# Row maxima and causal mask in one tile written by GpSimd, in a Flamingo block of cross-attention and mixture of experts

## The reference: what is computed

```python
q = proj(query, w_q, b_q); k = proj(key, w_k, b_k); v = proj(value, w_v, b_v)
scores = einsum('bhqd,bhkd->bhqk', q, k) / sqrt(D_K)
scores = where(mask, scores, -inf)            # mask: j <= i for sequences of 128
attn = softmax(scores, axis=-1)
out = einsum('bhqk,bhkd->bhqd', attn, v) ... @ w_o.T + b_o
x = x + tanh(g_xattn[0]) * out
x = x + tanh(g_ffn[0]) * experts(layernorm(x))
```

## Time and profile before

| | before |
|---|---|
| median of 3 runs | 963.27 us (963.25 to 963.42) |
| the profiled execution | 958.71 us, its span 956.9 us |
| granted clock of PE, mean | 0.952 |
| PE busy | 849.2 us (89%) |
| DVE busy | 603.9 us (63%) |
| ACT busy | 442.7 us (46%) |
| POOL busy | 258.1 us (27%) |
| mask product, L911 | 128 instructions, 49.1 us busy |

### The profile page before, as it was taken

The page is one execution under the profiler, slowest core; times in us unless marked ns, Lnnn a source line. Parts: engine busy times, 40 slices in busy tenths (PEclk is TensorE's granted clock), DMA queues, the critical chain, the costliest instruction groups (busy, mean ns, idle before and its releaser), DMA issues. The chain is left out here.

```text
span 956.9 us, 25073 instructions
## 1 busy us (share of the span) xinstructions
PE 849.2 (89%) x7600; PEld 752.0 (79%) x7601; DVE 603.9 (63%) x1521; ACT 442.7 (46%) x962; POOL 258.1 (27%) x239
## 2 busy tenths in 40 slices
PE   3699999999999999997258999999899989999990
PEld 2588888888888888886147888989799879889980
DVE  2458888888888888876625555555455545555550
ACT  2354555555555555554034454444445525544440
POOL 2101333323222233232301232332223322323222
PEclk9799999999999999998569999999999989999995
DMA  9767977878787878775878333233323322332212
GB/s 185 153 133 178 204 201 192 185 170 186 177 188 204 199 199 198 179 217 210 282 285 301 52 57 52 48 49 50 60 35 58 51 43 45 50 51 36 29 24 25
DMA packets 90231, 125.38 MB, mean 131 GB/s; under 512 B 13088, under 2 KB 81824, under 8 KB 85920
## 3 DMA queue, kind: packets, MB, share of 16 engines
q1 hardware_dynamic: 74752, 103.95, 42.3%
q0 software_dynamic: 14304, 19.15, 12.7%
q10 hardware_dynamic: 1088, 1.11, 0.4%
HBM read 55.21 MB, written 42.75 MB: 102 GB/s over the span
## 5 line engine op out<-in xcount | busy, mean ns | idle before, releaser
L1195 POOL DMA_INDIRECT out_rows<-yg,xs x78 | 126.6, 1623 | 349.7 <-ACT yg L1237 216.0
L1319 PE MATMUL bank<-xh,wts 128*128 128x256 f16 x1872 | 216.5, 277 | 0.0
L1335 PE MATMUL bank<-wts,hh 128*128 x1872 | 210.6, 273 | 0.0
L1319 PEld LDWEIGHTS bank<-xh,wts 128*128 x1872 | 186.2, 100 | 23.8
L1335 PEld LDWEIGHTS bank<-wts,hh 128*128 128x128 f16 x1872 | 183.2, 98 | 21.2
L1227 ACT ACTIVATE hf<-bank,b1t,gscale 128x256 f32<-128x256 f32 x312 | 154.9, 561 | 24.0 <-PE bank L1319 21.1
L935 PE MATMUL bank<-va,probs 128*128 128x102 f32 x1024 | 140.7, 279 | 7.9 <-DVE ao L653 7.9
L935 PEld LDWEIGHTS bank<-va,probs 128*128 128x128 f32 x1024 | 125.0, 193 | 10.6 <-DVE ao L653 7.4
L1237 ACT ACTIVATE yg<-yb,xs 128x256 f32<-128x256 f32 x78 | 35.4, 500 | 204.2 <-DVE yb L1276 183.1
L541 ACT ACTIVATE probs<-bank 128x512 f32<-128x512 f32 x128 | 76.8, 600 | 102.4 <-PE bank L918 96.7
L1266 DVE SCALAR_TENSOR_TENSOR hh<-hf,hscale,hh 128x512 f16<-128x512 f32 x156 | 117.2, 751 | 5.6
(11 more groups left out here) (169 smaller groups left out, 1108.2 us busy)
## 6 DMA issues: line engine op xcount, KB each, us to landing
wts<-in_W SPq DMA_DIRECT2D x16, 1024.0 KB, 8.0
split_weights<-wts SPq DMA_DIRECT2D x16, 1024.0 KB, 4.7
wts<-split_weights SPq DMA_DIRECT2D x16, 1024.0 KB
wts<-keys SPq DMA_DIRECT2D x96, 128.0 KB
wts<-queries SPq DMA_DIRECT2D x96, 128.0 KB
xs<-token_rows SPq DMA_DIRECT2D x39, 272.0 KB, 2.8
xin<-in_x SPq DMA_DIRECT2D x16, 256.0 KB, 5.0
cin<-in_ctx_in SPq DMA_DIRECT2D x16, 256.0 KB, 5.2
```

What stands on the lines that cost most here:

```text
L1195: pool.indirect_dma_start(out=out[:, :], out_offset=bass.IndirectOffsetOnAxis(ap=numbers, axis=0), in_=yg[m % 2][:, half, :], in_offset=No ...
L1319: last = pe.matmul(HB[c // 2][:, c % 2 * TILE:(c % 2 + 1) * TILE], wts[:, bass.ds(expert[1], 1), at:at + P], xh[b][:, xp, k, :], start=q = ...
L1335: last = pe.matmul(YB[b][:, half * D:(half + 1) * D], hh[b][:, hp, c, half * P:(half + 1) * P], wts[:, bass.ds(expert[0], 1), at:at + D], ...
```

## The change

- The product of L911 with its constants `ident16` and `maskT` goes. Each of the four slices of `TB` is now started by its own product with the cover.
- POOL writes, once for each quad, a `cover` of 128x4x128 bfloat16 (two buffers) with one `affine_select`: the row's maximum where the key is allowed, and 1e30 where it isn't. `cover` is the operand that, multiplied by `negident`, takes the maxima off.
- POOL's select is the first thing in each step; it waits for the row maxima of this quad, and for the transposed scores of quad n-2. PE waits for `cover_ready` in place of `max_ready`, and DVE's row maximum for `cover_ready` of quad n-2 in place of its transposed scores.
- The four scatters of a group move from steps 4, 5, 6, 7 to steps 3, 4, 6, 7.
- The covers lie in a tile `room` that the first stage otherwise doesn't use; `past`, which the routing table needs later, becomes a part of it.

```diff
-MASKED = -1e30
+MASKED = 1e30
...
-                step.later(pool.memset(maskT[:, :], 0.0))
...
-                pool.affine_select(out=maskT[:, :], in_=maskT[:, :], compare_op=ALU.is_ge,
-                                   fill=MASKED, base=0, pattern=[[1, P]],
-                                   channel_multiplier=-1).then_inc(consts, 1)
...
                 def it(g, par, half):
                     for n in range(QUADS):
+                        if there(g):
+                            pool.wait_ge(max_ready, g * QUADS + n + 1)
+                            settled(pool)
+                            when(pool, n >= 2 or there(g - 1), st_psum, g * QUADS + n - 1)
+                            settled(pool)
+                            pool.affine_select(out=cover[n % 2][:, :, :],
+                                               in_=rowmax[n % 2][:, :].unsqueeze(2).to_broadcast([P, 4, P]),
+                                               compare_op=ALU.is_ge, fill=MASKED, base=0, pattern=[[0, 4], [-1, P]],
+                                               channel_multiplier=1).then_inc(cover_ready, 1)
                         if n in (1, 5) and there(g - 1):
...
-                        if n >= 4 and there(g - 2):
-                            b, r = (n - 4) // 2, n % 2
-                            if n == 4:
+                        if n in (3, 4, 6, 7) and there(g - 2):
+                            b, r = divmod((3, 4, 6, 7).index(n), 2)
+                            if n == 3:
                                 pool.wait_ge(slots_ready, g - 1)
...
-                dve.tensor_copy(ident16[:, :], ident[:, :]).then_inc(dve_consts, 1)
...
                             dve.wait_ge(s_psum, g * QUADS + n + 1)
-                            when(dve, n >= 2 or there(g - 1), st_psum, g * QUADS + n - 1)
+                            when(dve, n >= 2 or there(g - 1), cover_ready, g * QUADS + n - 1)
...
-                            pe.wait_ge(max_ready, tg * QUADS + m + 1)
+                            pe.wait_ge(cover_ready, tg * QUADS + m + 1)
                             when(pe, m >= 2 or there(tg - 1), exp_ready, tg * QUADS + m - 1)
                             ps = TB[m % 2]
-                            pe.matmul(ps[:, :], ident16[:, :], maskT[:, :].unsqueeze(1).to_broadcast([P, 4, P]),
-                                      start=True, stop=False)
-                            for a in range(4):
-                                pe.matmul(ps[:, a * P:(a + 1) * P], rowmax[m % 2][:, a:a + 1].to_broadcast([P, P]),
-                                          negident[:, :], start=False, stop=False)
                             for a in range(4):
                                 h = 4 * (m % 4) + a
+                                pe.matmul(ps[:, a * P:(a + 1) * P], cover[m % 2][:, a, :],
+                                          negident[:, :], start=True, stop=False)
                                 last = pe.matmul(ps[:, a * P:(a + 1) * P], kst[i][:, h, tok],
-                                                 qst[i][:, h, tok], start=False, stop=a == 3)
+                                                 qst[i][:, h, tok], start=False, stop=True)
```

More of the change, by code:

```diff
@@ L127, in bass_flamingo @@
         negident = sb("negident", [P, P], BF16)
-        ident16 = sb("ident16", [P, P], BF16)
-        qsteps, ksteps, maskT = (sb(name, [P, P], BF16) for name in ("qsteps", "ksteps", "maskT"))
+        qsteps, ksteps = (sb(name, [P, P], BF16) for name in ("qsteps", "ksteps"))
         earlier = sb("earlier", [P, P], BF16)
@@ L154, in bass_flamingo @@
         tile_no = sb("tile_no", [1, ALL_TILES])
-        past = sb("past", [1, ALL_TILES, E])
+        room = sb("room", [P, ALL_TILES * E])
+        past = room[0:1, :].rearrange("p (t e) -> p t e", e=E)
         te, ts = sb("te", [1, ALL_TILES]), sb("ts", [1, ALL_TILES])
@@ L175, in attention_and_routing @@
     (x, ctx_in, g_xattn, g_ffn, w_q, b_q, w_k, b_k, w_v, b_v, w_o, b_o, W1, b1, W2, Wr, br, out,
-     xs_dram, w_dram, bank, qst, kst, qfull, kfull, ident, negident, ident16, qsteps, ksteps, maskT, earlier, ones16, rank1,
+     xs_dram, w_dram, bank, qst, kst, qfull, kfull, ident, negident, qsteps, ksteps, earlier, ones16, rank1,
      rank0, ones8, region0, base, mostsel, tgx, tgf, gates_in, power, wscale, wsquares, padrow,
@@ L180, in attention_and_routing @@
          "W1", "b1", "W2", "Wr", "br", "out", "xs_dram", "w_dram", "bank", "qst", "kst", "qfull", "kfull", "ident",
-         "negident", "ident16", "qsteps", "ksteps", "maskT", "earlier", "ones16", "rank1", "rank0", "ones8", "region0",
+         "negident", "qsteps", "ksteps", "earlier", "ones16", "rank1", "rank0", "ones8", "region0",
          "base", "mostsel", "tgx", "tgf", "gates_in", "power", "wscale", "wsquares", "padrow",
@@ L206, in attention_and_routing @@
         rowmax = [sb(f"rowmax{i}", [P, 4], BF16) for i in range(2)]
+        cover = [env["room"][:, 256 * i:256 * i + 256].bitcast(BF16).rearrange("p (a k) -> p a k", a=4)
+                 for i in range(2)]
         probs = [sb(f"probs{i}", [P, 4, P]) for i in range(4)]
@@ L253, in attention_and_routing @@
         v_psum, va_ready = sem("v_psum"), sem("va_ready")
-        s_psum, max_ready = sem("s_psum"), sem("max_ready")
+        s_psum, max_ready, cover_ready = sem("s_psum"), sem("max_ready"), sem("cover_ready")
         st_psum, exp_ready = sem("st_psum"), sem("exp_ready")
@@ L608, in _ @@
                 step.later(dve.memset(ones16[:, :], 1.0))
-                dve.wait_ge(consts, 9)
+                dve.wait_ge(consts, 8)
                 step.later(dve.tensor_copy(rank0[:, :], ints[:, 0, :]))
@@ L613, in _ @@
                 step.later(dve.tensor_copy(base[:, :], ints[:, 2, :]))
-                step.later(dve.tensor_scalar(negident[:, :], ident[:, :], -1.0, None, ALU.mult))
-                dve.tensor_copy(ident16[:, :], ident[:, :]).then_inc(dve_consts, 1)
+                dve.tensor_scalar(negident[:, :], ident[:, :], -1.0, None, ALU.mult).then_inc(dve_consts, 1)
                 step.wait()
```

## The result

The changed kernel takes 1035.6 us (median of 4 runs, 1033.1 to 1037.5) where the kernel before takes 963.3: ratio 1.077, 95% interval 1.073 to 1.080. That is 72 us more, where 26 were forecast and 1004 us was the end of the range. The direction was right, the size wrong by a factor of nearly three.

The account below looks back on a forecast made before the run. PE was taken to set the pace, with DVE deciding from step 4 to step 7. -1.05 + 1.5 + 0.62 + 0.8 = +1.87 us a group over 14 groups, +26 us, gave 989.5 us; range 970 to 1004 us.

Parts of the forecast that it names:

- Mask's product: PE's removed product saves 0.21 us each; five of eight a group count, the rest lie where PE waits: -1.05 us.
- Step 5: On POOL rs2 now stands behind cover(5), so DVE's norm2 starts later: +1.5 us a group, the dearest item.
- Step 6/7: cover(6) waits for DVE's L712 at the port, delaying ST(6) and PV(4): 0.62 us a group beyond the 1.5.
- Step 4: PE stalls for cover(3) ahead of ST(3): 0.8 us a group, lower bound 0.3, upper 1.6.
- upper bound's mechanism: In step 4's upper bound of 1.6 us, cover(2) also holds DVE's next two-input instruction for its 0.81 us.
- Groups 0 and 15 at zero: First and last attention groups lack one side of the pattern; taken as no change, within 1 us each.
- rival 1: No port conflict, the cover runs beside L712: +0.79 us a group, 974.3 us; chance 0.25.
- rival 3: Faster: in step 5 norm2 gets hold ahead of xb; 961 us, or 953 with a 0.5 us cover; chance 0.09.
- rival 2: Dearer: select takes 1.2 us, or covers hold DVE's two-input work in step 2; 1005.9 or 1000.7 us; chance 0.13.
- dearer cover: POOL's select takes 1.2 us, adding 0.39 in steps 4, 5 and 6: +3.04 us a group, 1005.9 us.
- Rival 4: Nothing: gain and loss cancel within 2 us, or PE's time went elsewhere than the removed product: 963 us; chance 0.04.
- groups of about 28 us: Sign expected in the profile after: an attention group takes about 28 us, where it took 26.0 before.

Follow-up runs that it names:

- kernel with its clock restored: The changed kernel with five and seven idle products on PE ahead of its waits for cover(5) and cover(6): 997.0 us, ratio 1.039.
- kernel with rs2 first: The changed kernel with POOL's rs2 of steps 1 and 5 moved ahead of the cover of that step: 980.3 us, ratio 1.021.

## Why the prediction was wrong, point by point

**The step that failed: PE's work was priced at the clock of before.** The prediction read "a granted clock of 1.00" in its first stretch and then summed every term at that clock, PE's own as -1.05 us, while the same sum put up to 2.9 us more of waits (1.5 + 0.62 + 0.8) into PE's program per group. That these waits could take the clock down stood in none of the terms and none of the rivals. It was worth 39 us, 1035.6 - 997.0, of the 72. The Trainium skill, "TensorE: Matmul & The Clock Gate", section "Part 1: The HAM clock gate", says that activity releases PE's full clock and that idling brings the lower one back. The runs agree: 39 us less with idle products in the waits, at a clock of 1.00. Whether these waits were enough for a fall, no row of the kernel before tells; but it was a rival to be named.

**The sum of the waits was about right**, 1.87 us a group forecast, 2.0 measured at full clock. That is in part luck, since errors in its terms cancel. What was measured of them makes -1.03 + 1.53 + 0.34 + 0.93 = 1.77; the other 0.24 us stay open. The terms:

- *Mask's product, -1.05*: measured alone, -1.03. Five of eight was right.
- *Step 5, +1.5*: measured 1.53. The cover is cheaper than taken (0.62, not 0.81), the way to it longer (0.33, not 0.1); the two errors cancel. That the step was the dearest item is shown by the order of its two instructions, worth 55 us alone, and 26 us where the clock is 1.00 both times.
- *Step 6/7*: ST(6) comes 1.21 us after rowmax(6), 1.52 forecast. The cover does wait for the weights' split, but for 0.2 us only, since the 0.33 us of start-up lie beside it. In the kernel with idle products the value product comes 1.68 us after rowmax(6) has ended, before it was 1.34: 0.34 more, where the term had 0.62.
- *Step 4, 0.8*: in the kernel with idle products PE waits 0.59 us for the heads in step 3 and 0.34 for cover(3) (from start to start), 0.93. The upper bound's mechanism, a cover that holds DVE's next two-input instruction, was real, at 0.44 us.
- *Groups 0 and 15 at zero*: wrong. In the changed kernel norm2 waited 5.3 us at the end of attention for a scatter to land, and the prediction had not followed the scatter of step 7 behind cover(7). In the kernel with idle products these waits were 5.9 us, in the kernel before 0.6, a difference of 5.3; with 14 x 2.0 = 28 us this makes 33 of the 35.5 us between the two (997.0 - 961.5).

**The rivals.** The port conflict exists (rival 1 falls). xb won against norm2 again, 1.36 us, and nothing was faster (rival 3 falls). Of rival 2, the dearer cover (1005.9 us) was not so: 0.62 us. Its other half, covers that hold DVE's two-input work in step 2, is real, at 0.44 us for the 0.81 it took; its 1000.7 us lie near the 997 of the kernel with its clock restored, but the clock was no part of it. Rival 4 falls too: the mask's product alone was worth 11.7 us.

**What the prediction said would show it** came for the most part: norm2 1.5 us late, PE waiting for POOL, 1.27 and 1.70 us ahead of ST(5) and ST(6). Ahead of ST(3) it was 0.17 us, not 1 to 1.5, and a cover beside the port's other user took 0.83 us, not 1.4. Its mark "groups of about 28 us" held for the kernel with the clock restored, 28.34, and failed for the change, 31.12.

## What to carry to other kernels

Before trusting a sum on PE, add up the waits that the change puts into its densest stretch: here, with 3.3 us of waits in 5.7 us, the clock then ran at half for 7 to 10 us in ten groups of eleven, and the price doubled (72 us against the 35.5 of the kernel with its clock restored), while with 0.9 us at the same place it had not fallen. Idle products in the waits are a cheap test of this, if each is put exactly where PE waits. When work moves to an engine with time to spare, what stands behind it in that engine's program costs as much as the work itself: put it last in its step, behind what others wait for, and only for the pieces whose consumer comes late.

## What was not expected of the hardware

- The same wait doesn't always end in the same clock: in the kernel with rs2 first PE waits 1.81 us ahead of ST(5) in each group, and some groups run at 1.00 and others at 0.94. In the changed kernel one group of eleven kept its clock through the same waits as the others. So the fall can be looked for from such waits, not counted from them.
- A select of 128x512 bfloat16 on POOL takes 0.62 us undisturbed, twice the 0.30 of 128x128, not four times.
- Two-input instructions of DVE are held by a POOL instruction that reads SBUF even when that reads few bytes: L770 took 0.72 us beside a cover whose input is four values a partition, 0.28 without. That is the rule of the Trainium skill, "SBUF — State Buffer", section "Who interferes with whom", weighed in the prediction, in the one place where I had left it to the upper bound. The row of the changed kernel, from the groups by line, 40 to 440 us:

```profile
L770 DVE TENSOR_TENSOR sel<-sel,pos 128x128 f32<-128x128 f32 x12 | 8.6, 720 | 0.0
```
